# Sources of the cells kept as rows by the first mean pass and loaded by the later ones

## The chip, the cores and the metric

The kernel runs on one core of a Trainium2 chip. The metric is the device time of one execution in microseconds. A core has TensorE (PE in the rows; its weight loads are PEld), VectorE (DVE), ScalarE (ACT), GpSimd (POOL) and the queue engine SyncE (SP), which only issues DMAs here. TensorE's clock has two levels, 1.2 and 2.4 GHz; the granted clock is given as a share of the higher.

## The reference

A graph of 6,250 nodes with 64 features and 206,250 edges sorted by destination goes through four residual blocks, each followed by a layer norm. The first is three mean (SAGE) layers, the second two weighted sums, the third one elementwise sum, the fourth three attention layers. The change touches the three mean layers:

```python
def _sage_conv(x, src, dst, ea, Wl, bl, Wr):
    msg = jax.nn.relu(x[src] + ea)
    s = jax.ops.segment_sum(msg, dst, num_segments=N)
    cnt = jax.ops.segment_sum(jnp.ones((msg.shape[0],), msg.dtype), dst, num_segments=N)
    agg = s / jnp.maximum(cnt, 1.0)[:, None]
    return agg @ Wl + bl + x @ Wr
```

Here ea is edge_attr_16 @ emb_ea, the same in all three layers.

## The kernel before

Nodes are numbered so that source s lies in partition s // 52, column s mod 52 of a table X (later Y) in SBUF. `sage_pass` handles one mean layer. The edges are cut into groups of 896; four groups make a block of destinations. For most edges no row is gathered: the first pass ("sage0", `first_pass` true, 46 blocks) scatters each edge's embedded attributes and its metadata into "bins" in DRAM, one bin for each column of sources, with 112 slots (SL). A *piece* is four such bins (PC = 4) and a block has 13 pieces (NPC = 13). The later passes ("sage1", "sage2", 33 blocks each) read the same bins, and take three further groups a block ("plain" groups) by gathering rows with GpSimd. The first pass has one plain group a block, sums the wide attributes for the third residual block ("aux" events in bodies 2, 4, 6, 9, 11), and does the binning of a block two ahead: binning products in bodies 1, 4, 7, 10 on TensorE, with `pack` on ScalarE, and on VectorE `split` in body 0 and `place` in body 2. It also builds and stores the adjacency that the second residual block uses.

The steps of piece q, body by body of the same loop on every engine (each engine follows its own written order and waits on semaphores):

- ScalarE, `cells_load` (line 1199): the piece's cells (112 slots x 4 bins x 68 words) come from the bins, six pieces ahead (ring RR = 6).
- TensorE, `spread_cells` (line 891): a cell holds the partition of its source, plus 1, as a bf16 number. Four matmuls against the identity put the row of all 448 of them onto all 128 partitions of one of two PSUM banks. In body q the spread of piece q+2 stands in front of everything else.
- VectorE, `near_cells` (line 1034): compares that with the number of the partition and gives the 0/1 matrix `near` (ring R = 3). It stands in body q-1 for piece q, in front of the join.
- TensorE, `fetch` (line 899): four matmuls of `near` and the node table put each cell's source row into PSUM. It waits for near q and for earlier joins (one bank in the first pass, two in the later).
- VectorE, `far_cells` (1038), `join` (1043: fetched rows plus attributes) and, in the first pass, `turned_cells` (1048).
- ScalarE: `rectify` (1204), in the first pass `weigh` (1190, four instructions, needs the join and the turned cells) and `keep` (1210 and its DMA issue 1212) for the adjacency of piece q-2, then the load of the cells of piece q+6.
- TensorE: in the first pass `adjacency` (908) of piece q-2, and `add_cells` (918), which sums the cells of the last pieces. These are gathered in flushes: bodies 0, 3, 7 and 12 of the first pass, 3, 7 and 12 of the later ones.

A plain group (`plain_event`: body 5 in the first pass, 1, 5 and 9 later) adds a product for its attributes (932) and its sums (944) on TensorE, a choice matrix (1062) and a sum (1065) on VectorE in front of that body's join, and a rectifying on ScalarE. SyncE's queue loads sources and attributes.

The first pass's order on ScalarE, in each body:

```python
rectify(qn, s)
if first_pass:
    weigh(qn, k, s)
    if i > 1:
        keep(b, u, it, i - 2)
    elif not (isinstance(b, int) and b == 0):
        keep(*after(b, u, it, -1), NPC + i - 2)
if not (isinstance(b, int) and qn + RR >= pieces):
    cells_load(*spot(b, u, it, i, RR))
```

Of the kernel before, what the change touches and what calls it, by code (L numbers as in the profile page):

```python
# [8 lines left out]
B16 = mybir.dt.bfloat16  # L9
# [5 lines left out]
P = 128  # L15
# [96 lines left out]
def build(nc, A, out):  # L112
    ctx = ExitStack()
    with ctx:
# [12 lines left out]
        adj = dram("adj", (NBK, P, TS * MW))  # L127

# [80 lines left out]
        def lay(region, sizes):  # L209

            at, rings = 0, []
            for n, size in sizes:
# [8 lines left out]
        attr_later = lay(work[:], [(R, PC * SL), (RR, P)])[1]  # L221
# [50 lines left out]
        s_bA = [sem(f"bufA_loaded{i}") for i in range(R)]  # L272
# [9 lines left out]
        s_block = [sem(f"block_loaded{i}") for i in range(2 * NGC)]  # L282
        names = ["bad_counted", "bad_summed", "ids_split", "bins_hot", "bins_counted", "meta_ready", "ranked", "slot_ready", "bin_ea_ready", "pay_ready",
                 "spread", "near_ready", "fetched", "joined", "cells_ready", "far_hot_ready", "weighed", "turned_ready", "adj_ready",
# [462 lines left out]
        def sage_pass(name, table, nodes, B, per, first_pass=False):  # L747
# [5 lines left out]
            ea_banks = [bank[0]]  # L753
# [33 lines left out]
            with nc.Block() as block:  # L787
                @block.sync
                def _(sp):
# [28 lines left out]

                    def body(b, u, it):
                        ahead = after(b, u, it, LEAD)  # L820
                        for i in range(NPC):
                            if first_pass:
# [10 lines left out]
                    if first_pass:  # L833
                        for b in range(LEAD):
                            source_load(b, b)
                            for r in range(GB):
                                bin_load(b, r)
                    for j in range(per):
# [46 lines left out]
                def _(pe):  # L885
                    def spread_cells(qn, b, u, it, i):

                        s, lap = laps(NPC, u, it, i, RR)
                        wait(pe, (s_pays[s], 16 * lap + 16), (q["near_ready"], qn - 1))
# [5 lines left out]
                    def fetch(qn, k, i):  # L895
# [117 lines left out]
                    spread_cells(0, 0, 0, 0, 0)  # L1013
                    spread_cells(1, 0, 0, 0, 1)
# [13 lines left out]
                def _(ve):  # L1028
# [3 lines left out]
                    def near_cells(qn, k):  # L1032
                        wait(ve, (q["spread"], qn + 1), (q["fetched"], qn - R + 1))
                        nc.vector.tensor_scalar(near[k % R], spread[k % 2][:, 0:PC * SL], part1[:], None, ALU.is_equal).then_inc(q["near_ready"].handle, 1)  # L1034
# [97 lines left out]
                    def body(b, u, it):  # L1132
                        ahead = after(b, u, it, LEAD)
                        for i in range(NPC):
# [5 lines left out]
                            if not (isinstance(b, int) and qn == pieces - 1):  # L1140
                                near_cells(qn + 1, k + 1)
# [14 lines left out]
                            if first_pass:  # L1156
                                turned_cells(qn, k, s)

# [5 lines left out]
                    near_cells(0, 0)  # L1164
# [14 lines left out]
                def _(ac):  # L1179
# [33 lines left out]

                    def pack(b, u, r):
# [11 lines left out]
                    def body(b, u, it):  # L1226
# [3 lines left out]
                        for i in range(NPC):  # L1230
# [7 lines left out]
                            if first_pass:  # L1238
# [3 lines left out]
                                elif not (isinstance(b, int) and b == 0):  # L1242
                                    keep(*after(b, u, it, -1), NPC + i - 2)
# [1113 lines left out]
```

## Time and profile before

| | us |
|---|---|
| median of 3 runs | 14045.62 |
| lowest and highest | 14029.52, 14058.77 |
| profiled execution, its own time | 14037.41 |
| span of its profile | 14035.6 |
| mean granted TensorE clock | 0.698 of full |

The page gives busy times over the span and, in 40 slices of 351 us each, busy shares and the granted clock in tenths. Rows of the timeline begin with the start and the duration in us; a bracket at the end says how long the engine was idle before and what released it. Some rows stand for several instructions ("x4"); an f32 matmul counts as two.

### The profile page before, as it was taken

The numbers are of one execution on the slowest core, as the hardware profiler recorded it, in microseconds if no ns is written. First come the engines' busy times: TensorE is split into PE (matmuls) and PEld (weight loads), VectorE is DVE, ScalarE is ACT, GpSimd is POOL, SyncE is SP. The second block draws the span as 40 slices with busy tenths as digits, with TensorE's granted clock in tenths as the row PEclk, the third lists the DMA queues.
The fourth block names the chain that finished last, engine by engine and source line by source line (L and its number), as shares of the span: only waits on it lengthen the run. The fifth ranks groups of instructions, "written<-read, shape, count | busy, mean of one in ns | idle before, by whom it ended". The sixth has DMA issues, their size and how long they took to land. (4 is left out here: it accounts for less than half of the span.)

```text
span 14035.6 us, 291323 instructions
## 1 busy us (share of the span) xinstructions
PE 10475.4 (75%) x76483; PEld 9348.2 (67%) x76484; DVE 8592.3 (61%) x23645; ACT 4454.9 (32%) x9519; POOL 8334.0 (59%) x8516
## 2 busy tenths in 40 slices
PE   5888888888888988788875666666666666666665
PEld 4777777777887878688864555554555554555554
DVE  6666666666656656511136666666666666666666
ACT  2444444441111111100013333333333333333333
POOL 5555555535553645353516777774777774777773
PEclk9988888897988888899975555555555555555555
DMA  4444444432222222376743433332443332443332
GB/s 126 143 140 137 138 143 137 139 112 64 66 64 60 67 63 64 92 256 214 253 137 82 96 94 95 95 94 62 94 95 94 95 94 62 95 95 94 95 94 53
DMA packets 1180716, 1506.22 MB, mean 107 GB/s; under 512 B 379416, under 2 KB 906803, under 8 KB 1179290
## 3 DMA queue, kind: packets, MB, share of 16 engines
q10 hardware_dynamic: 367424, 691.34, 15.4%
q0 software_dynamic: 272384, 301.97, 12.2%
q1 hardware_dynamic: 539610, 498.60, 12.0%
q8 instruction: 448, 7.34, 0.2%
q14 instruction: 850, 6.96, 0.2%
HBM read 1212.18 MB, written 278.84 MB: 106 GB/s over the span
## 5 line engine op out<-in xcount | busy, mean ns | idle before, releaser
L1991 POOL DMA_INDIRECT rows<-gat_table,idx x2457 | 2361.4, 961 | 1309.1 <-issue 747.9
L1991 POOL DMA_INDIRECT Y<-gat_table,idx x2394 | 2305.7, 963 | 729.6 <-issue 729.6
L867 POOL DMA_INDIRECT rows<-node_table,idx x1386 | 1337.9, 965 | 1342.6 <-DVE msg L1065 633.2
L855 POOL DMA_INDIRECT bins<-scratch,slots x1288 | 1336.4, 1038 | 1228.0 <-DVE slots L1115 498.4
L918 PE MATMUL bank<-xT 112*64 112x120 f32 (+1 forms) x11648 | 1575.5, 305 | 0.0
L918 PEld LDWEIGHTS bank<-xT 112*64 112x64 f32 (+1 forms) x11648 | 1513.0, 164 | 17.3
L1204 ACT ACTIVATE xT<-xT 112x256 f32<-112x256 f32 x1456 | 604.2, 415 | 2892.8 <-DVE xT L1043 2526.8
L2005 PE MATMUL scores<-ident,rep 128*128 128x128 f32 x2436 | 600.9, 424 | 1123.1 <-ACT rep L2096 826.8
L2005 PE MATMUL scores<-ident,scratch 128*128 128x128 f32 x2415 | 595.8, 424 | 1075.3 <-ACT scratch L2096 863.0
L2050 PE MATMUL bank<-sel,msg 128*72 128x32 f32 x9702 | 1308.7, 309 | 0.0
L2005 PEld LDWEIGHTS scores<-ident,rep 128*128 128x128 f32 x2436 | 471.6, 222 | 1169.5 <-issue 1169.5
L2050 PEld LDWEIGHTS bank<-sel,msg 128*72 128x72 f32 x9702 | 1215.8, 237 | 44.4
L2005 PEld LDWEIGHTS scores<-ident,scratch 128*128 128x128 f32 x2415 | 467.6, 222 | 1121.5 <-issue 1121.5
L2152 DVE CUSTOM_DVE_ANT_0 work<-scores,work 128x896 f32<-128x896 f32 x1041 | 1108.0, 1089 | 104.5 <-PE scores L2005 23.0
L1043 DVE TENSOR_TENSOR xT<-scores,xT 112x256 f32<-112x256 f32 x1028 | 434.9, 423 | 1081.7 <-PE scores L899 1053.2
L1327 POOL DMA_INDIRECT rows<-node_table,idx x658 | 623.1, 947 | 769.0 <-DMA idx<-in_src 280.9
L1038 DVE TENSOR_TENSOR xT<-counts,xT 112x480 f32<-112x480 f32 x1456 | 949.3, 652 | 203.7 <-PE bank L918 168.4
L1034 DVE TENSOR_SCALAR work<-scores,part 128x448 f32<-128x448 f32 x1456 | 987.9, 678 | 34.3 <-PE scores L891 34.3
L908 PE MATMUL bank<-xT,work 112*128 112x120 f32 x4784 | 791.0, 317 | 212.0 <-ACT work L1210 178.3
L908 PEld LDWEIGHTS bank<-xT,work 112*128 112x128 f32 x4784 | 702.3, 223 | 350.3 <-issue 343.9
L899 PE MATMUL scores<-X,work 128*112 128x64 f32 x4784 | 654.0, 286 | 255.1 <-issue 250.0
L891 PE MATMUL scores<-ident,xT 112*128 112x112 bf16 x5824 | 556.6, 221 | 301.7 <-DVE work L1034 182.5
(249 smaller groups left out, 21439.8 us busy)
## 6 DMA issues: line engine op xcount, KB each, us to landing
work<-in_dst_rows SPq DMA_DIRECT2D x693, 448.0 KB
xT<-bins ACTq DMA_DIRECT2D x1456, 119.0 KB
adj<-work ACTq DMA_DIRECT2D x598, 240.0 KB
work<-adj ACTq DMA_DIRECT2D x184, 780.0 KB, 4.4
xT<-adj ACTq DMA_DIRECT2D x184, 780.0 KB
bins<-zeros ACTq DMA_DIRECT2D x46, 1547.0 KB, 8.2
work<-in_attr SPq DMA_DIRECT2D x231, 224.0 KB
work<-in_dst_rows SPq DMA_DIRECT2D x693, 64.0 KB
```

The source lines that it names most:

```text
L855: nc.gpsimd.indirect_dma_start(bins, bass.IndirectOffsetOnAxis(slots[u % 2][:, r * G + j:r * G + j + 1], 0), binf[r][:, j, :], None).then_ ...
L867: nc.gpsimd.indirect_dma_start(rows[s][:, k, 0:D], None, table, bass.IndirectOffsetOnAxis(idx[s][:, k:k + 1], 0)).then_inc(s_rows[s].handl ...
L899: last = nc.tensor.matmul(joint[k % JR][0:SL, c * D:(c + 1) * D], near[k % R][:, c * SL:(c + 1) * SL], nodes[:, i * PC + c, :], start=True ...
L908: last = nc.tensor.matmul(adj_sum[:, c * MW:(c + 1) * MW], turned[k % R][0:SL, c * P:(c + 1) * P], far_hot[k % RR][0:SL, c * MW:(c + 1) * ...
L918: last = nc.tensor.matmul(sums[u % SR][0:width, 0:MW], cellf[k % RR][0:SL, c, 0:width], far_hot[k % RR][0:SL, c * MW:(c + 1) * MW], start= ...
L1034: nc.vector.tensor_scalar(near[k % R], spread[k % 2][:, 0:PC * SL], part1[:], None, ALU.is_equal).then_inc(q["near_ready"].handle, 1)
L1038: nc.vector.tensor_tensor(far_hot[s][0:SL, :].rearrange("p (c m) -> p c m", m=MW), bc(counts[0:SL, 1:MW + 1], [SL, PC, MW], 1), bc(payf[s] ...
L1327: nc.gpsimd.indirect_dma_start(rows[s][:, k, 0:D], None, table, bass.IndirectOffsetOnAxis(idx[s][:, k:k + 1], 0)).then_inc(s_rows[s].handl ...
L1991: nc.gpsimd.indirect_dma_start(rows[s][:, j, :], None, gat_table, bass.IndirectOffsetOnAxis(idx[s % RR][:, j:j + 1], 0)).then_inc(s_rows[s ...
L2005: last = nc.tensor.transpose(score_banks[s % 2][:, j * P:(j + 1) * P], reps[s % 2][:, j, :], ident[:])
L2050: last = nc.tensor.matmul(wide[s % 2][0:ROW, 0:WIN], msg[s % R][:, j, :], sel[s % R][:, j, :], start=j == 0, stop=j == G - 1)
L2152: nc.vector.tensor_tensor_reduce(out=fars[s % 2][k], in0=score_banks[s % 2][:, 0:GE], in1=fars[s % 2][k], scale=1.0, scalar=-3.0e38, op0=A ...
```

## The change

The first pass copies, for each piece, partition 0 of the spread bank as bf16 to SBUF on ScalarE (`keep_row`) and stores that row (448 numbers of two bytes, 896 bytes) to a new DRAM tensor `sources`. The bank may be spread over only when its row is copied: `spread_cells` waits for `row_out_ready` too. The copy for piece q+1 stands in ScalarE's body q behind `keep` and in front of the cells' load.

The later passes have no `spread_cells`. SyncE's queue loads the stored row onto all 128 partitions (`row_load`, ring of six, issued when near q-6 is done), and `near_cells` reads it from SBUF. It now stands behind the join of body q, for piece q+2. The freed PSUM bank becomes a second bank for the plain groups' attribute products. The rest is bookkeeping of semaphores.

```diff
+        sources = dram("sources", (NBK, TS * SL // 2))
...
+        kept_row = [work[0:1, (3 * R - 1) * GE + i * PC * SL // 2:(3 * R - 1) * GE + (i + 1) * PC * SL // 2] for i in range(R)]
+        attr_later, row = lay(work[:], [(R, PC * SL), (RR, P), (RR, PC * SL // 2)])[1:]
...
-            ea_banks = [bank[0]]
+            ea_banks = [bank[0]] if first_pass else [bank[0], bank[1]]
...
+                    def row_load(b, u, it, i):
+                        qn = NPC * b + i
+                        s, lap = laps(NPC, u, it, i, RR)
+                        wait(sp, (q["near_ready"], qn - RR + 1))
+                        sp.dma_start(row[s], sources[ds(b, 1), i * PC * SL // 2:(i + 1) * PC * SL // 2].broadcast_to([P, PC * SL // 2])
+                                     ).then_inc(s_row[s].handle, 16)
...
                         for i in range(NPC):
+                            if not first_pass and not (isinstance(b, int) and NPC * b + i + RR >= pieces):
+                                row_load(*spot(b, u, it, i, RR))
...
-                        wait(pe, (s_pays[s], 16 * lap + 16), (q["near_ready"], qn - 1))
+                        wait(pe, (s_pays[s], 16 * lap + 16), (q["near_ready"], qn - 1), (q["row_out_ready"], qn - 1))
...
-                            if not (isinstance(b, int) and qn + 2 >= pieces):
+                            if first_pass and not (isinstance(b, int) and qn + 2 >= pieces):
                                 spread_cells(qn + 2, *spot(b, u, it, i, 2))
-                            fetch(qn, k, i)
+                            fetch(qn, b, u, it, i)
...
-                        wait(ve, (q["spread"], qn + 1), (q["fetched"], qn - R + 1))
-                        nc.vector.tensor_scalar(near[k % R], spread[k % 2][:, 0:PC * SL], part1[:], None, ALU.is_equal).then_inc(q["near_ready"].handle, 1)
+                        wait(ve, (q["spread"], qn + 1) if first_pass else (s_row[s], 16 * lap + 16), (q["fetched"], qn - R + 1))
+                        found = spread[k % 2][:, 0:PC * SL] if first_pass else row[s].bitcast(B16)
+                        nc.vector.tensor_scalar(near[k % R], found, part1[:], None, ALU.is_equal).then_inc(q["near_ready"].handle, 1)
...
                             far_cells(qn, s, lap)
-                            if not (isinstance(b, int) and qn == pieces - 1):
-                                near_cells(qn + 1, k + 1)
+                            if first_pass and not (isinstance(b, int) and qn == pieces - 1):
+                                near_cells(qn + 1, *spot(b, u, it, i, 1))
...
                             join(qn, k, s)
                             if first_pass:
                                 turned_cells(qn, k, s)
+                            elif not (isinstance(b, int) and qn + 2 >= pieces):
+                                near_cells(qn + 2, *spot(b, u, it, i, 2))
...
+                    def keep_row(b, u, it, i):
+                        qn, k = NPC * b + i, NPC * u + i
+                        s, lap = laps(NPC, u, it, i, R)
+                        wait(ac, (q["near_ready"], qn + 1), (s_row_kept[s], 16 * lap))
+                        nc.scalar.activation(kept_row[s].bitcast(B16), spread[k % 2][0:1, 0:PC * SL], ACT.Copy).then_inc(q["row_out_ready"].handle, 1)
+                        wait(ac, (q["row_out_ready"], qn + 1))
+                        ac.dma_start(sources[ds(b, 1), i * PC * SL // 2:(i + 1) * PC * SL // 2], kept_row[s]).then_inc(s_row_kept[s].handle, 16)
...
                                     keep(*after(b, u, it, -1), NPC + i - 2)
+                                if not (isinstance(b, int) and qn == pieces - 1):
+                                    keep_row(*spot(b, u, it, i, 1))
                             if not (isinstance(b, int) and qn + RR >= pieces):
                                 cells_load(*spot(b, u, it, i, RR))
```

## Rows read from the trace of the kernel before

**Rows 1.** The page: busy times over the span; granted TensorE clock by slice.

```profile
PE 10475.4 (75%) x76483; PEld 9348.2 (67%) x76484; DVE 8592.3 (61%) x23645; ACT 4454.9 (32%) x9519; POOL 8334.0 (59%) x8516
...
PEclk9988888897988888899975555555555555555555
```

**Rows 2.** Line 1034 in each mean pass: min/median/max ns, first and last start.

```profile
L1034 DVE TENSOR_SCALAR work<-scores,part x598: 670/679/684, 123.4 to 3095.0; 128x448 f32<-128x448 f32 x200
...
L1034 DVE TENSOR_SCALAR work<-scores,part x429: 670/679/683, 3221.1 to 4493.2; 128x448 f32<-128x448 f32 x143
...
L1034 DVE TENSOR_SCALAR work<-scores,part x429: 668/679/685, 4539.3 to 5834.6; 128x448 f32<-128x448 f32 x143
```

**Rows 3.** Timeline of TensorE in a block of the first pass: start, duration.

```profile
1513.67 1.71 PE L899 MATMUL scores<-X,work 128*112 128x64 f32 x8
1515.32 1.70 PE L977 MATMUL bank<-scratch,work 128*64 128x32 f32 x14
1516.95 2.06 PE L908 MATMUL bank<-xT,work 112*128 112x120 f32 x8
1518.81 0.58 PE L891 MATMUL scores<-ident,xT 112*128 112x112 bf16 x4
1519.18 1.71 PE L899 MATMUL scores<-X,work 128*112 128x64 f32 x8
1521.13 2.03 PE L908 MATMUL bank<-xT,work 112*128 112x120 f32 x8 [0.24 <-ACT work L1210]
...
1526.84 0.96 PE L899 MATMUL scores<-X,work 128*112 128x64 f32 x8
```

**Rows 4.** Timeline of VectorE in that block: joins of bodies 0, 2, 3, 4, 12, 0.

```profile
1507.86 0.42 DVE L1043 TENSOR_TENSOR xT<-scores,xT 112x256 f32<-112x256 f32 x1 [0.26 <-DVE Y L1108]
...
1518.00 0.42 DVE L1043 TENSOR_TENSOR xT<-scores,xT 112x256 f32<-112x256 f32 x1 [0.17 <-DVE maxrank L1117]
...
1521.07 0.42 DVE L1043 TENSOR_TENSOR xT<-scores,xT 112x256 f32<-112x256 f32 x1 [0.37 <-PE scores L899]
...
1527.98 0.42 DVE L1043 TENSOR_TENSOR xT<-scores,xT 112x256 f32<-112x256 f32 x1 [4.72 <-PE scores L899]
...
1559.84 0.43 DVE L1043 TENSOR_TENSOR xT<-scores,xT 112x256 f32<-112x256 f32 x1 [3.29 <-PE scores L899]
...
1573.89 0.42 DVE L1043 TENSOR_TENSOR xT<-scores,xT 112x256 f32<-112x256 f32 x1 [0.26 <-DVE Y L1108]
```

**Rows 5.** Timeline of ScalarE in body 2 of that block.

```profile
1519.15 1.28 ACT L1190 ACTIVATE work<-work,xT 112x128 f32<-112x128 f32 x4 [0.18 <-DVE work L1048]
1520.33 0.55 ACT L1210 ACTIVATE work<-bank 128x480 f32<-128x480 f32 x1
1521.12 0.37 ACTq L1212 DMA_DIRECT2D adj<-work  x1
1521.73 0.33 ACTq L1199 DMA_DIRECT2D xT<-bins  x1
```

**Rows 6.** Windows of that block: length, busy PE, PEld, DVE, ACT, POOL, clock, DMA, GB/s.

```profile
1516.00:1520.00 4.00, 4.00 (x27) 3.89 (x26) 3.79 (x7) 1.27 (x4) 1.28 (x1) 0.50 0.54 160
...
1552.00:1556.00 4.00, 2.94 (x35) 2.79 (x35) 3.02 (x7) 2.58 (x8) 1.39 (x1) 1.00 0.35 108
1556.00:1560.00 4.00, 3.93 (x21) 3.72 (x22) 0.68 (x3) 2.04 (x6) 2.87 (x3) 0.52 0.63 192
```

**Rows 7.** Timeline of TensorE in a block of the second mean pass.

```profile
4200.80 0.37 PE L891 MATMUL scores<-ident,xT 112*128 112x112 bf16 x4
...
4206.93 0.36 PE L891 MATMUL scores<-ident,xT 112*128 112x112 bf16 x4 [1.14 <-DVE work L1034]
...
4208.01 5.16 PE L918 MATMUL bank<-xT 112*64 112x120 f32 x32
```

**Rows 8.** Timeline of VectorE in the same stretch.

```profile
4205.20 0.42 DVE L1043 TENSOR_TENSOR xT<-scores,xT 112x256 f32<-112x256 f32 x1
...
4206.11 0.68 DVE L1034 TENSOR_SCALAR work<-scores,part 128x448 f32<-128x448 f32 x1
```

More of the change, by code:

```diff
@@ L271, in build @@
         s_idx = [sem(f"idx_loaded{i}") for i in range(RR)]
-        s_bA = [sem(f"bufA_loaded{i}") for i in range(R)]
+        s_bA = [sem(f"bufA_loaded_or_row_kept{i}") for i in range(R)]
+        s_row_kept = s_bA
         s_rows = [sem(f"rows_loaded{i}") for i in range(GR)]
@@ L281, in build @@
         s_kept = [sem(f"adjacency_kept{i}") for i in range(R)]
-        s_block = [sem(f"block_loaded{i}") for i in range(2 * NGC)]
+        s_block = [sem(f"stored_piece_loaded{i}") for i in range(2 * NGC)]
+        s_row = s_block[0:RR]
         names = ["bad_counted", "bad_summed", "ids_split", "bins_hot", "bins_counted", "meta_ready", "ranked", "slot_ready", "bin_ea_ready", "pay_ready",
-                 "spread", "near_ready", "fetched", "joined", "cells_ready", "far_hot_ready", "weighed", "turned_ready", "adj_ready",
+                 "spread", "row_out_ready", "near_ready", "fetched", "joined", "cells_ready", "far_hot_ready", "weighed", "turned_ready", "adj_ready",
                  "adj_out_ready", "cells_summed", "accumulated", "auxsel_ready",
@@ L837, in _ @@
                                 bin_load(b, r)
+                    else:
+                        for i in range(RR):
+                            row_load(0, 0, 0, i)
                     for j in range(per):
@@ L893, in spread_cells, with fetch @@
                         last.then_inc(q["spread"].handle, 1)
-                    def fetch(qn, k, i):
+                    def fetch(qn, b, u, it, i):
+                        k = NPC * u + i
                         wait(pe, (q["near_ready"], qn + 1), (q["joined"], qn - JR + 1))
@@ L1012, in _ @@
                                 bin_event(b, b, r)
-                    spread_cells(0, 0, 0, 0, 0)
-                    spread_cells(1, 0, 0, 0, 1)
+                        spread_cells(0, 0, 0, 0, 0)
+                        spread_cells(1, 0, 0, 0, 1)
                     over_blocks(body, B)(pe.Fori)
@@ L1163, in _ @@
                             place(b, b)
-                    near_cells(0, 0)
+                    near_cells(0, 0, 0, 0, 0)
+                    if not first_pass:
+                        near_cells(1, 0, 0, 0, 1)
                     over_blocks(body, B)(ve.Fori)
@@ L1254, in _ @@
                         cells_load(0, 0, 0, i)
+                    if first_pass:
+                        keep_row(0, 0, 0, 0)
                     over_blocks(body, B)(ac.Fori)
@@ L1264, in _ @@
                             ac.wait_ge(s_kept[i].handle, s_kept[i].at(16 * slot_total(i, R, pieces)))
+                            ac.wait_ge(s_row_kept[i].handle, s_row_kept[i].at(16 * slot_total(i, R, pieces)))
             for s in range(RR):
@@ L1269, in sage_pass @@
                 s_pays[s].done(16 * slot_total(s, RR, pieces))
+                if not first_pass:
+                    s_row[s].done(16 * slot_total(s, RR, pieces))
             for s in range(AR):
                 s_attr[s].done(16 * slot_total(s, AR, n1))
-            for x in ["spread", "near_ready", "fetched", "joined", "cells_ready", "far_hot_ready", "cells_summed"]:
+            for x in (["spread", "row_out_ready"] if first_pass else []) + ["near_ready", "fetched", "joined", "cells_ready", "far_hot_ready", "cells_summed"]:
                 q[x].done(pieces)
@@ L1279, in sage_pass @@
                     s_kept[s].done(16 * slot_total(s, R, pieces))
+                    s_row_kept[s].done(16 * slot_total(s, R, pieces))
                 s_ve.done((6 + 3 + 3) * B)
```

5 lines of the change are left out of this document (3 added, 2 removed).

## The prediction

> **What bounds the kernel now.** I read the page first [rows 1]: TensorE is busy for 75% of the span, and its granted clock is near full in the first 18 slices, which hold the three mean passes, and at half in the attention passes behind them, which the change leaves alone. Then I dated the passes by the instruction that finds the near cells, line 1034 [rows 2]: 598 pieces from 123 to 3095 us in the first pass, 429 from 3221 to 4493 in the second, 429 from 4539 to 5835 in the third. That is 64.6 us for each of the 46 blocks of the first pass and 38.5 and 39.2 us for each of the 33 blocks of the others. The rest of the forecast is about what a block costs.
>
> Next I laid one block of the first pass beside its engines. The joins (line 1043, VectorE) are the mark to count by, one for each piece: 1507.86 is body 0 and 1573.89 is body 0 of the next block, 66.0 us [rows 4]. No engine bounds it throughout. From body 12 to body 0 (1559.84 to 1573.89, 14.05 us [rows 4]) VectorE is at the split; in the bodies that flush, TensorE is at its sums (to body 4's fetch, 1519.18 to 1526.84 [rows 3]); in the others the four engines hand a piece on in about 3 us. What makes 3 us possible is that the engines work on different pieces: TensorE spreads piece q+2 and fetches q while ScalarE is still weighing q-1.
>
> In a later block TensorE has nearly all the time, but with a wait: it spreads piece 7 at 4206.93 only when near (line 1034) has let it, after 1.14 us idle [rows 7].
>
> **The change in the first pass.** Every piece gets a copy of one row to SBUF on ScalarE and one more DMA issue. That ScalarE has room (32% of the span busy [rows 1]) is not the question; the new wait is. TensorE may spread piece q+2 only when ScalarE has copied piece q's row (two spread banks), and it does so ahead of fetch q. ScalarE copies row q at the end of its body q-1: behind the rectify, the weighing and the keeping of that body, all of which hang on join q-1, which hangs on fetch q-1. So fetch q now waits for a chain that begins with fetch q-1, and the pieces no longer overlap. The loop, from join to join:
> - join to weigh start, 1518.00 to 1519.15: 1.15 [rows 4, 5]
> - weigh to keep, 1519.15 to 1520.33: 1.18 [rows 5]
> - keep to its DMA issue, to 1521.12: 0.79 [rows 5]
> - from there to the next slot, where now the cells' load is issued (1521.73) and where the row's copy will stand: 0.61 [rows 5]
> - the copy, 448 elements a partition out of PSUM: the nearest row is the keep's 480, 0.55; the one partition saves nothing that I count [rows 5]
> - to TensorE's next start: keep's end (1520.33 + 0.55) to the adjacency at 1521.13, 0.25 [rows 3, 5]
>
> Sum 4.53 us from a join to the next spread. Then spread to fetch, 0.37 at half clock (1518.81 to 1519.18 [rows 3]), 0.2 at full; fetch to join 1.89 at half (1519.18 to 1521.07) and 1.14 at full (1526.84 to 1527.98) [rows 3, 4]. Join to join is 5.87 us at full clock and 6.79 us at half, where it was about 3. The copy's own DMA issue and the cells' load behind it take some 1.4 us more (0.79 and 0.61 again) and end before the next rectify can start, so they cost nothing; if the chain were shorter than 4 us they would.
>
> A block has 13 such gaps. The one from body 12 to body 0 stays 14.05: the split needs only the spread of piece 1 and the first sums of the flush, and both come as before.
> - All at full clock: 12 x 5.87 + 14.05 = 84.5, and an estimated 2.5 for the placing and the plain group, which hold VectorE longer than a loop: 87 us.
> - All at half: 12 x 6.79 + 14.05 = 95.5. In seven bodies an aux or binning product lies between fetch and adjacency: fetch 1513.67, aux 1515.32, adjacency 1516.95 for 2.06 [rows 3], so keep can begin 3.28 + 2.06 + 0.25 = 5.6 us behind the fetch, not 1.89 + 2.33 = 4.22: 7 x 1.4 = 9.6. The flushes of bodies 3 and 7 hold TensorE beyond the loop (1519.18 to a spread at 1526.84 - 0.2, 7.46 us against 1.89 + 4.53 = 6.4 [rows 3]), about 1 and 3 us, less 1.8 as the clock is up behind them; the plain group 2. Together 109 us.
>
> Which clock? From 1516 to 1520 TensorE was busy all 4 us and still had 0.50; between 1552 and 1556 it was busy 2.94 of 4 and the next stretch has 0.52 [rows 6]. In the new loop a body outside the flushes gives TensorE half of 0.37 + 1.65 + 2.06, with an aux product half of 1.63 more [rows 3]: 2.0 to 2.9 us of work at full clock in 5.9, a smaller share than in the stretch ahead of that fall. I take half clock for about four gaps in five, the flushes lifting it for a body or so: 109 - 0.2 x 22 = 104 to 105, say 104. Less 66.0 is 38 us a block, and x 46 that is **+1750 us**. Bounds: +21 a block at full clock (+970); +50 (+2300) if the falls also reach what I leave unchanged.
>
> The clock is also where a rule of the skill gives another sum. The Trainium skill, TensorE: Matmul & The Clock Gate, section "HAM oscillation", lays a lost clock at gaps of idleness longer than one that it names, and the gaps of this loop would stay just under it; by it the block would be the 87 us one. This trace doesn't bear it out where the clock falls behind a stretch that was three quarters busy, so it stays a rival.
>
> The 598 stores are one row of 896 bytes each, and their slot is waited for only three pieces later, some 18 us; nothing.
>
> **The change in the later passes.** Each piece loses its four spreading matmuls and gains a load on SP's queue, asked for six pieces ahead (over 15 us), so I take it as hidden; the group loads behind it on that queue now go out about one block ahead rather than as soon as their slot is free, and a block is 35 us: hidden too. If the load came late, near would wait for DMA, and I have no row for its landing; by the bound of the cells' load, which has as many bytes and is six ahead too, nothing shows. Near goes behind the join and two pieces ahead. VectorE has the same instructions; near's source is now SBUF, priced as before.
>
> One group of four bodies now takes from 4200.80 to 4208.01, 7.21 us [rows 7]. Without spreads TensorE's work up to fetch 6 is over 0.6 us sooner. The last fetch then waits for near 7: the join of 5 at 4205.20 [rows 8] comes 0.4 sooner (two spreads), near starts 0.34 behind it, as far did, instead of 0.91 (4206.11 [rows 8]), and takes 0.68; the old wait ran 0.82 from near's start (4206.11 to 4206.93 [rows 7, 8]) and a spread of 0.2. So flush starts at 7.21 - 0.4 - 0.57 - 0.2 = 6.04. That is 1.17 less a group, 3.5 a block, and x 66 blocks **-230 us**. Bounds: 0, if the clock takes it back; -420, if all 13 spreads and the waits of 1.14 go (6.4 x 66).
>
> **Sum.** +1750 - 230 = +1520. On the profiled execution (span 14035.6, its time 14037.4) that is 15,560; the median of the runs shown is 8 us above it, which is nothing here. **15,560 us.**
>
> **The rivals.**
> - *The loop at full clock*, or at a good part of it: +970 - 230, from about 14,750 up to 15,300. For it: flushes lift the clock quickly. Against: [rows 6]. 27%.
> - *The copy is absorbed* (the other side): ScalarE is idle for about half of those stretches [rows 6], and if the row's copy came in that idle time without TensorE waiting for it, the first pass would stay and 230 us be won: 13,800. It would decide so wherever the wait on the copy is met before the join of the same body. Against: the copy's place in ScalarE's order, behind rectify and keep. 7%.
> - *Worse than the half-clock loop*: the block nearer 116, or nothing won later on: above 16,050. 6%.
> - *No effect*, by the two halves cancelling: they differ by seven times. 1%.
> - *My forecast*, loop mostly at half clock: 15,300 to 16,050. 59%.
>
> **How the numbers follow.** The range 14,750 to 16,050 holds the forecast's own and the full-clock rival's cases, about 85 in 100; what is left out is the other side and the worst case. 0.2% (28 us) is about what a measurement of this kernel can tell from no change. Slower by more than that 0.92, within it 0.01, faster 0.07.
>
> **What would show it.** Right: joins of the first pass 6 to 8 us apart outside the split; TensorE's spread (line 891's successor) idle in front, released by ScalarE's new copy, some 2 to 3 us each in 598; the first pass ending near 4840 us; clock there down from 8 or 9 tenths to 6 or 7; later blocks near 35.5 us with no 1.14 us waits. Wrong: a spread that waits for nothing; a first pass that ends where it did; later passes that wait for the row's DMA. What would make the sum wrong with the mechanism right is the clock, by up to 700 us.

## Result, and the profile after

Before 14,047.67 us (14,029.52 to 14,058.77, 4 runs), after 15,402.83 us (15,399.27 to 15,407.38, 4 runs): 1.0966 times before, 95% interval 1.0947 to 1.0985, or 1355 us slower. The forecast was 15,560.

The page after, first the busy times, then the granted clock by slice, as [rows 1]:

```profile
PE 11014.5 (72%) x73051; PEld 9786.3 (64%) x73052; DVE 8385.4 (54%) x23645; ACT 4820.0 (31%) x10117; POOL 8307.6 (54%) x8516
...
PEclk7666666666666998998999655555555555555555
```

TensorE has 3,432 matmuls fewer and is busy for 539 us longer: its work was done at a lower clock. The 12 slices at 6 tenths lie in the first pass. Line 1055 (near cells, line 1034 before) in the three passes, to set against [rows 2]; min/median/max ns, first and last start:

```profile
L1055 DVE TENSOR_SCALAR work<-scores,part x598: 669/676/684, 123.2 to 4856.0; 128x448 f32<-128x448 f32 x200
...
L1055 DVE TENSOR_SCALAR work<-work,part x429: 435/444/552, 4988.5 to 6072.1; 128x448 f32<-128x448 bf16 x143
...
L1055 DVE TENSOR_SCALAR work<-work,part x429: 436/444/642, 6117.1 to 7194.2; 128x448 f32<-128x448 bf16 x143
```

From first to last near cells the passes take 4732.8, 1083.6 and 1077.1 us, against 2971.6, 1272.1 and 1295.3. That is +1761 in the first pass and -188.5 and -218.2 in the later ones, in sum +1354 of the 1362 us between the two profiled spans: almost the whole difference lies here.

How the +1761 of the first pass splits for TensorE is in its windows, with the second pass below. First the kernel before, then after; columns are length, busy us (instructions) of PE, PEld, DVE, ACT, POOL, granted clock, DMA share, GB/s:

```profile
123.00:3095.00 2972.00, 2491.22 (x20990) 2286.74 (x20988) 2025.19 (x3777) 1351.65 (x3969) 1675.53 (x1586) 0.87 0.47 139
3221.00:4493.00 1272.00, 1142.40 (x10087) 1033.50 (x10087) 778.32 (x1611) 234.66 (x526) 670.98 (x693) 0.88 0.28 65
```

```profile
123.00:4856.00 4733.00, 3328.44 (x20985) 3017.78 (x20984) 2031.39 (x3777) 1714.51 (x4565) 1574.73 (x1586) 0.64 0.28 87
4988.00:6072.00 1084.00, 1001.92 (x8376) 894.20 (x8377) 671.67 (x1610) 234.52 (x525) 705.17 (x693) 0.91 0.54 122
```

The same 21,000 matmuls of the first pass are busy for 3328 us instead of 2491 (+837: the clock went from 0.87 to 0.64), and TensorE is idle for 1405 us instead of 481 (+924: the wait).

The loop itself, from one join to the next (after, the timeline of all engines; start and duration in us, in brackets the idle time before):

```profile
1935.57 0.42 DVE L1064 TENSOR_TENSOR xT<-scores,xT 112x256 f32<-112x256 f32 x1 [4.37 <-PE scores L917]
...
1936.73 1.28 ACT L1215 ACTIVATE work<-work,xT 112x128 f32<-112x128 f32 x4 [0.18 <-DVE work L1069]
...
1936.96 2.06 PE L926 MATMUL bank<-xT,work 112*128 112x120 f32 x8
...
1939.17 0.57 ACT L1235 ACTIVATE work<-bank 128x480 f32<-128x480 f32 x1 [1.17 <-PE bank L926]
1939.98 0.36 ACTq L1237 DMA_DIRECT2D adj<-work  x1
1940.62 0.53 ACT L1243 ACTIVATE work<-scores 1x448 bf16<-1x448 f32 x1 [0.87 <-ACT work L1235]
...
1941.25 0.53 PE L907 MATMUL scores<-ident,xT 112*128 112x112 bf16 x4 [2.23 <-issue]
...
1941.57 1.71 PE L917 MATMUL scores<-X,work 128*112 128x64 f32 x8
...
1943.46 0.42 DVE L1064 TENSOR_TENSOR xT<-scores,xT 112x256 f32<-112x256 f32 x1 [5.48 <-PE scores L917]
```

Join to weigh 1.16, weigh to keep 2.44 (1.17 of it a wait for the adjacency product), keep to its DMA issue 0.81, to the copy 0.64, copy to spread 0.63, spread to fetch 0.32, fetch to join 1.89: 7.89 us, each step in the place that the prediction gave it (6.79, and 1.4 more where an aux or binning product lies between, as here). The gap before this one, from a join at 1929.02, has no wait for the adjacency and is 6.55.

### The profile page after: what moved, and what is told of

It reads as the page before. It is cut to its first block and busy times, and to the rows that moved or that the text cites. A ratio compares the mean times of both kernels' runs of the same rounds, so it can differ in the third digit from the quotient of the medians.

```text
span 15397.5 us, 290993 instructions
## 1 busy us (share of the span) xinstructions
PE 11014.5 (72%) x73051; PEld 9786.3 (64%) x73052; DVE 8385.4 (54%) x23645; ACT 4820.0 (31%) x10117; POOL 8307.6 (54%) x8516
## 5 line engine op out<-in xcount | busy, mean ns | idle before, releaser
L871 POOL DMA_INDIRECT bins<-scratch,slots x1288 | 1282.4, 996 | 3000.3 <-ACT scratch L1251 1575.2
L883 POOL DMA_INDIRECT rows<-node_table,idx x1386 | 1410.3, 1018 | 933.8 <-DMA idx<-in_src 508.3
L936 PE MATMUL bank<-xT 112*64 112x120 f32 (+1 forms) x11648 | 1540.3, 300 | 0.0
L907 PE MATMUL scores<-ident,xT 112*128 112x112 bf16 x2392 | 280.9, 260 | 1413.3 <-issue 1112.5
L907 PEld LDWEIGHTS scores<-ident,xT 112*128 112x128 bf16 x2392 | 180.0, 116 | 1519.6 <-issue 1518.4
L926 PEld LDWEIGHTS bank<-xT,work 112*128 112x128 f32 x4784 | 975.9, 296 | 156.8 <-issue 143.1
L926 PE MATMUL bank<-xT,work 112*128 112x120 f32 x4784 | 1054.3, 392 | 1.0 <-ACT work L1235 1.0
L1368 POOL DMA_INDIRECT rows<-node_table,idx x658 | 624.2, 949 | 723.8 <-DVE msg L1417 247.8
L917 PE MATMUL scores<-X,work 128*112 128x64 f32 x4784 | 890.3, 356 | 0.0
```

Of the source, the lines that this page charges most:

```text
L871: nc.gpsimd.indirect_dma_start(bins, bass.IndirectOffsetOnAxis(slots[u % 2][:, r * G + j:r * G + j + 1], 0), binf[r][:, j, :], None).then_ ...
L883: nc.gpsimd.indirect_dma_start(rows[s][:, k, 0:D], None, table, bass.IndirectOffsetOnAxis(idx[s][:, k:k + 1], 0)).then_inc(s_rows[s].handl ...
L917: last = nc.tensor.matmul(joint[k % JR][0:SL, c * D:(c + 1) * D], near[k % R][:, c * SL:(c + 1) * SL], nodes[:, i * PC + c, :], start=True ...
L926: last = nc.tensor.matmul(adj_sum[:, c * MW:(c + 1) * MW], turned[k % R][0:SL, c * P:(c + 1) * P], far_hot[k % RR][0:SL, c * MW:(c + 1) * ...
L936: last = nc.tensor.matmul(sums[u % SR][0:width, 0:MW], cellf[k % RR][0:SL, c, 0:width], far_hot[k % RR][0:SL, c * MW:(c + 1) * MW], start= ...
L1368: nc.gpsimd.indirect_dma_start(rows[s][:, k, 0:D], None, table, bass.IndirectOffsetOnAxis(idx[s][:, k:k + 1], 0)).then_inc(s_rows[s].handl ...
```

## Experiments

**One copy, three places in ScalarE's order.** The first run moves the copy, with its store, to the head of ScalarE's body, ahead of pack, rectify and weigh; all else of the change stays.

```diff
                             s, lap = laps(NPC, u, it, i, RR)
+                            if first_pass and not (isinstance(b, int) and qn == pieces - 1):
+                                keep_row(*spot(b, u, it, i, 1))
                             if first_pass and i in at_bin and binned_ahead(b):
...
-                                if not (isinstance(b, int) and qn == pieces - 1):
-                                    keep_row(*spot(b, u, it, i, 1))
```

> The changed kernel with one thing moved: ScalarE copies and stores the row of piece q+1 first in its body q, ahead of packing, rectifying and weighing; the same work, off the chain that begins with the join. If the loop through the copy is the cost (first pass 123 to 4856 us in the changed kernel, 102.9 us a block), the loop is gone and only some 1.3 us more of ScalarE's work in each body is left, which shows in the dense bodies: about 72 us a block, first pass ending near 3450 us, total 13,900 to 14,050. If ScalarE's added work itself, or the store, is the cost, nothing moves: 15,400.

Measured 14,066.81 us, 1.0006 times before (0.9997 to 1.0016): no difference from before, 8.7% less than the change as made, and 17 us above the range expected. The first pass takes 3392 us instead of 4733, the later passes 1084.0 and 1083.2, as after. The 1341 us hang on one place in an order. The second run puts the same two lines between weigh and keep.

```diff
                                 weigh(qn, k, s)
+                                if not (isinstance(b, int) and qn == pieces - 1):
+                                    keep_row(*spot(b, u, it, i, 1))
...
                                     keep(*after(b, u, it, -1), NPC + i - 2)
-                                if not (isinstance(b, int) and qn == pieces - 1):
-                                    keep_row(*spot(b, u, it, i, 1))
```

> The copy of the row between weighing and keeping: still behind the join, but the chain is shorter by keep, its DMA issue and the way to the copy, 0.79 + 0.58 = 1.37 us a body, and by the wait of keep for the adjacency where there is one. If the loop is the cost: 12 bodies x 46 blocks x 1.37 = 760 us less, up to 1200 with those waits, a little less where a flush holds TensorE: 14,300 to 14,800. If the work is the cost, or if only being ahead of the join helps: 15,400.

Measured 14,532.14 us, 1.0341 times (1.0312 to 1.0370); first pass 3847 us, clock 0.70. The nearer the copy stands to the head of the body, the shorter the pass: 4733, 3847, 3392.

**More work, no more waiting.** If the price were ScalarE's own time, more of it would cost more. This run has ScalarE copy 448 zeros on one partition twice more in each body of the first mean pass, behind the cells' load, where nothing on TensorE waits for it; nobody reads the result.

```diff
+                    ac_spare = work[0:1, 3 * R * GE - PC * SL // 2:3 * R * GE].bitcast(B16)
...
                                 cells_load(*spot(b, u, it, i, RR))
+                            if first_pass:
+                                for n in range(2):
+                                    wait(ac, (s_ac, 2 * qn + n))
+                                    nc.scalar.activation(ac_spare, zeros[0:1, 0:PC * SL], ACT.Copy).then_inc(s_ac.handle, 1)
```

> The changed kernel with two further one-partition copies of 448 numbers on ScalarE behind the cells' load of every body of the first pass (about 1.2 us, more than the row's copy with its issue adds); nobody waits for them. If the wait and not the work is the cost, they fall into ScalarE's idle 1.5 to 2 us ahead of the next rectify: 15,400, within 0.4%. If ScalarE's work is the cost: 598 x 1.2 = +700, 16,100.

Measured 15,414.5 us, 1.0974 times (1.0946 to 1.1002), as after. Its windows of the first pass:

```profile
124.00:4855.00 4731.00, 3330.65 (x20983) 3021.90 (x20983) 2031.18 (x3776) 2391.43 (x5757) 1570.41 (x1585) 0.64 0.29 87
```

ScalarE is busy for 677 us more (2391 against 1715) and the pass is no longer: ScalarE's throughput is not what costs.

**How much is the clock.** TensorE gets 24 small matmuls (bf16, 64 columns, into a bank nobody reads) ahead of its wait for the copy, in 11 of 13 bodies: the wait stays, but TensorE is busy in part of it.

```diff
+FILL = 24
...
+                        if (i + NPC - 2) % NPC not in (9, 10) and not (isinstance(qn, int) and qn < 13):
+                            for _ in range(FILL):
+                                nc.tensor.matmul(bank[6][:, 448:512], ident16[:], ident16[:, 0:64], start=True, stop=True)
                         wait(pe, (s_pays[s], 16 * lap + 16), (q["near_ready"], qn - 1), (q["row_out_ready"], qn - 1))
```

> The changed kernel with 24 small bf16 matmuls (64 columns) into unused columns of the plain groups' bank ahead of the wait of each spread in the first pass, in 11 of 13 bodies; their result is read by nobody. It asks how much of the 102.9 us a block is TensorE's lower clock (0.63 of full in a block of the changed kernel). If the fillers hold the clock up, a block falls towards the 87 us of the full-clock sum, less what they cost where nothing is waited for: 92 to 98 us, total 14,900 to 15,200. If the clock stays at half whatever is done, they add their own time in the flushing bodies: 15,450 to 15,700.

Measured 15,199.22 us, 1.0816 times (1.0786 to 1.0846), at the upper end of what was expected.

```profile
124.00:4650.00 4526.00, 3476.03 (x32861) 3214.99 (x32861) 2033.90 (x3777) 1714.22 (x4565) 1606.88 (x1585) 0.73 0.30 91
```

With 11,900 matmuls more the pass is 206 us shorter, at a clock of 0.73 instead of 0.64. So the clock is a price of its own beside the wait. By the prediction's blocks of 87 and 109 us full against half clock would be 1012 us over 46 blocks. The clock rose by 0.09 of the 0.50 that lie between the two levels, which would be 182 us, estimated, and 206 were found, the filler's own time included. A clock near full was not reached, so the whole share of the clock stays an estimate.

**The later passes: order or spreads.** They gained 407 us where 230 were forecast. The first run puts near cells back in front of the join, one piece ahead, as before the change; row loads stay, spreads stay away.

```diff
-                            if first_pass and not (isinstance(b, int) and qn == pieces - 1):
+                            if not (isinstance(b, int) and qn == pieces - 1):
                                 near_cells(qn + 1, *spot(b, u, it, i, 1))
...
-                            elif not (isinstance(b, int) and qn + 2 >= pieces):
-                                near_cells(qn + 2, *spot(b, u, it, i, 2))
...
-                    if not first_pass:
-                        near_cells(1, 0, 0, 0, 1)
```

> The changed kernel with near of the later passes back where it was, one piece ahead and in front of the join; the row still comes from SBUF and there are no spreads. It asks what the order is worth of the 406 us that the two later passes fell (1272 to 1084 and 1295 to 1077 us from first to last near). The prediction's account gives the order 0.57 us a group of bodies, 198 groups: +110 us, 15,510. If the order is worth nothing (TensorE bound): 15,400.

Measured 15,611.19 us, 1.1102 times (1.1085 to 1.1119). The later passes are 1173.5 and 1180.2 us, 193 more than after: the order is worth 193, not the 110 expected. How much the passes as changed vary by themselves, six profiles show: in the change and in the five runs that leave these passes alone and in which the kernel before took its 14,050 us, their sum lies between 2160.7 and 2178.5 us. The 193 are against the lowest of them. The second run has TensorE make the spreads in the later passes as before, with no wait on near or copy; nobody reads them.

```diff
-            ea_banks = [bank[0]] if first_pass else [bank[0], bank[1]]
+            ea_banks = [bank[0]]
...
-                        wait(pe, (s_pays[s], 16 * lap + 16), (q["near_ready"], qn - 1), (q["row_out_ready"], qn - 1))
+                        wait(pe, (s_pays[s], 16 * lap + 16), *([(q["near_ready"], qn - 1), (q["row_out_ready"], qn - 1)] if first_pass else []))
...
-                            if first_pass and not (isinstance(b, int) and qn + 2 >= pieces):
+                            if not (isinstance(b, int) and qn + 2 >= pieces):
                                 spread_cells(qn + 2, *spot(b, u, it, i, 2))
```

> The changed kernel with the four spreading matmuls a piece still made in the later passes and read by nobody (and one bank for the plain groups' attributes, as before the change); near reads the row from SBUF, in its new place. If TensorE's time is most of the gain: 858 x 0.2 = +170 us, up to +240 with the half clock in part of it: 15,570 to 15,640. If the gain is all in VectorE's shorter near and the order: within 40 us of 15,400.

Measured 15,392.19 us, 1.0943 times (1.0927 to 1.0960): the first case, with TensorE's time as most of the gain, is a miss; the time measured is that of the second. The later passes take 1077.9 and 1064.2, in sum 2142, 19 us less than the lowest of the six without the spreads. Why, the groups of TensorE in the second pass show; first before, then after, then this run (matmuls, busy us, mean ns, idle before them):

```profile
L918 PE MATMUL bank<-xT 112*64 112x120 f32 x3384 | 480.3, 315 | 0.0
...
L891 PE MATMUL scores<-ident,xT 112*128 112x112 bf16 x1712 | 160.0, 217 | 128.6 <-DVE work L1034 90.5 <-issue 37.7 <-DMA xT<-bins 0.3
```

```profile
L936 PE MATMUL bank<-xT 112*64 112x120 f32 x3384 | 425.2, 292 | 0.0
L917 PE MATMUL scores<-Y,work 128*112 128x64 f32 x1712 | 219.8, 274 | 47.6 <-DVE work L1055 39.6 <-issue 8.0
L917 PE MATMUL bank<-Y,work 128*112 128x64 f32 x1710 | 218.8, 273 | 39.1 <-DVE work L1055 39.1
```

```profile
L936 PE MATMUL bank<-xT 112*64 112x120 f32 x3384 | 374.4, 270 | 0.0
L917 PE MATMUL scores<-Y,work 128*112 128x64 f32 x1719 | 212.6, 268 | 14.0 <-DVE work L1055 11.3 <-issue 0.2
L917 PE MATMUL bank<-Y,work 128*112 128x64 f32 x1712 | 211.4, 268 | 19.0 <-DVE work L1055 17.1
L907 PE MATMUL scores<-ident,xT 112*128 112x112 bf16 x1712 | 160.2, 216 | 17.5 <-issue 16.5 <-DMA xT<-bins 1.0
```

The spreads fill stretches in which TensorE else waits for near (idle before the fetches 87 us after, 33 here), and the same 3384 products of the sums take 270 ns instead of 292: the clock is 0.97 in these passes, 0.91 and 0.92 after. In the second pass TensorE is busy for 76 us more outside the sums, 51 less in them, and idle for 31 less. In this order a spread costs nothing.

**A version faster than before?** The next three runs start from the copy at the head. The first has SyncE issue the row's store, one piece ahead, behind the attribute loads of its body.

```diff
+                    def row_store(b, u, it, i):
...
+                        wait(sp, (q["row_out_ready"], qn + 1))
+                        sp.dma_start(sources[ds(b, 1), i * PC * SL // 2:(i + 1) * PC * SL // 2], kept_row[s]).then_inc(s_row_kept[s].handle, 16)
...
+                            if first_pass and not (isinstance(b, int) and NPC * b + i == pieces - 1):
+                                row_store(*spot(b, u, it, i, 1))
...
-                        wait(ac, (q["row_out_ready"], qn + 1))
-                        ac.dma_start(sources[ds(b, 1), i * PC * SL // 2:(i + 1) * PC * SL // 2], kept_row[s]).then_inc(s_row_kept[s].handle, 16)
```

> The copy first in the body, as in the experiment that only moves it, and the store's DMA issued by SyncE's queue and not by ScalarE's, which saves ScalarE about 0.5 us a body. If ScalarE's work shows in dense bodies once the loop is gone: 80 to 200 us below that experiment, 13,750 to 13,900. If ScalarE is not the bound there: no difference.

Measured 14,075.53 us, 1.0012 times (1.0003 to 1.0021): no difference from the copy at the head, whose first pass took 3392 us and this one's 3396. But two waits for late attributes, which that run does not have, appear in its list of waits between 500 and 3000 us (total, times, longest):

```profile
PE bank L1005 <- DMA work<-in_attr: 176.2, 98, 2.6
...
PE scores L996 <- DMA work<-in_attr: 51.0, 37, 2.0
```

SyncE, it seems, now stands at the store's wait, and the attribute loads behind it go out late. The next run issues each store five bodies later, when its copy is long done:

```diff
+                            if first_pass and not (isinstance(b, int) and NPC * b + i < 4):
+                                row_store(*spot(b, u, it, i, -4))
...
+                    if first_pass:
+                        for i in range(NPC - 4, NPC):
+                            row_store(B - 1, (B - 1) % UB, (B - 1) // UB, i)
```

> The copy first in ScalarE's body and the store on SyncE's queue, but five pieces further back in that queue's order, so that the attribute loads behind it go out early again (with the store one piece ahead TensorE waited 1.5 to 2.3 us at 1567.55, 1588.07, 1592.71 and 1619.86 for DMA of the attributes). If those waits ate what ScalarE's shorter body saved: first pass about 3150 to 3280 us instead of 3396, total 13,800 to 13,950, faster than the kernel before. If ScalarE's 0.5 us a body is worth nothing: as before the move, 14,060.

It ran, with two of those below, on chip 13, on which the kernel before itself took 18,076 us instead of 14,050, so these are compared only with each other and with that. It took 18,287.22 us, 1.0124 times (1.0101 to 1.0148). The same kernel once more, on chip 6:

> The kernel with the copy first and the store five pieces back on SyncE's queue, once more, since in its first call the kernel before itself took 18,076 us and not 14,047. As expected then: first pass about 3150 to 3280 us, total 13,800 to 13,950, if the late attribute loads ate what ScalarE's shorter body saved; 14,060 if that half microsecond is worth nothing.

There before took 18,368 us and it took 18,550.16, 1.0101 times (1.0078 to 1.0125). The waits for the attributes are gone from the list of waits of the same stretch, as the reading of SyncE's queue wants it, but others, which the trace puts down to no instruction of the core, stand on VectorE (up to 16.4 us) and ScalarE (up to 14.5), with the other engines behind them:

```profile
DVE xT L1075 <- remote: 838.0, 86, 16.4
```

On both of these chips it is 1% slower than the kernel before; what it takes on one without such waits stays open. No version here was shown to beat the kernel before.

**What is left of the later passes.** Near reads bf16 from SBUF now and takes 0.444 us instead of 0.678. This run cuts it in two halves of 0.331 each in the later passes, together about the old duration; all else is as in the change.

```diff
+                            half_row = PC * SL // 2
+                            nc.vector.tensor_scalar(near[k % R][:, 0:half_row], found[:, 0:half_row], part1[:], None, ALU.is_equal)
+                            nc.vector.tensor_scalar(near[k % R][:, half_row:], found[:, half_row:], part1[:], None, ALU.is_equal).then_inc(q["near_ready"].handle, 1)
```

> The changed kernel with near of the later passes in two instructions of 224 columns, which brings its time on VectorE from 0.44 back to about the 0.68 us that it took from PSUM; place and order as changed. If near's price is on the path (TensorE waits 79 us a pass for it in the changed kernel, 130 times): two nears a group, 198 groups, 0.2 us each: +40 to +80 us, 15,440 to 15,490. If it is hidden: 15,400.

Measured 19,675.74 us, 1.0874 times (1.0841 to 1.0908). It ran on chip 13. Here and in the next two runs the passes are dated from first to last join. Its later passes take 3168.7 us; those of the store-behind run on the same chip, which are the change's own, 3142.7: +26 for the old duration, less than the 40 to 80 expected. The same passes took 3219.4 on chip 6, and the six runs of the store-behind kernel on chip 13 lie up to 155 us apart, so 26 from one profile each can't be told from nothing. The last two are one kernel, run on chip 13 and on chip 6, with the two edits shown above, near back in its old place and the spreads made:

> Both at once: spreads of the later passes still made, and near back in its old place; what is left of the change there is near's source (SBUF, 0.44 instead of 0.68 us, and no wait on a spread). The later passes took 2567 us before, 2354 with near in the old place and no spreads, 2142 with near in the new place and spreads made, 2161 as changed. If the spreads cost nothing in either order, the later passes take about 2350 and the total is 15,600; if they cost TensorE's 0.2 us a piece when it waits for near more often: 2350 + 170, total 15,780.

> Near in its old place and the spreads still made, once more for the same reason. If the spreads cost nothing in either order, the later passes take about 2350 us and the total is 15,600, and what is left of the gain, some 210 us, belongs to near's source (0.44 instead of 0.68 us, and no wait on a spread); if they cost TensorE's 0.2 us a piece: 2350 + 170, total 15,780.

Measured 19,825.67 us, 1.0965 times (1.0940 to 1.0991), and 20,088.61, 1.0935 times (1.0910 to 1.0961). Against the store-behind kernel on the same chip the later passes take +220 and +173 us, where the old place alone cost 193: with near in its old place too the spreads cost about nothing. What they do cost is within the 25 or so by which these two miss 193 on either side, and that is no more than the noise here.

## Why the prediction was right, and where its sizes were off

**The loop: right, and shown.** Moving the copy with its store, and nothing else, gives back 1341 of the 1761 us; more work on ScalarE costs nothing. In the block read above joins lie 6.5 to 9.1 us apart outside the split: the ten gaps from 1905.24 to 1981.88 average 7.66 us, and the gap at the split is 13.80 against 14.05. A block takes 102.9 in the mean against 104 forecast, and the pass ends at 4856 against 4840. TensorE's wait in front of the spread is there, but the trace names "issue" for most of it. The groups of the first pass after, TensorE's spread and ScalarE's copy:

```profile
L907 PE MATMUL scores<-ident,xT 112*128 112x112 bf16 x2389 | 280.6, 260 | 1404.6 <-issue 1112.5 <-ACT work L1243 292.0
```

```profile
L1243 ACT ACTIVATE work<-scores 1x448 bf16<-1x448 f32 x596 | 317.7, 533 | 480.0 <-ACT work L1235 462.9 <-issue 13.8 <-DVE work L1055 3.3
```

All 1405 us of TensorE's idle time stand before the spread. Forecast were 2 to 3 us at each of the 598; 465 spreads waited, 3.0 us each in the mean, and the others found TensorE at work, so it is 2.3 us a piece over all. Only 292 are put down to the copy. The timeline settles it: 457 of the 465 start within 0.3 us behind a copy's end, most of them 0.1 (1941.15 and 1941.25 above), and the runs that move the copy move the idle time. The copy's price, too, was right: one partition of 448 elements takes 0.53 us, as 480 on 128 partitions take 0.56.

**The clock: right.** Windows of the same block after, and the row of TensorE that the fall belongs to:

```profile
1920.00:1922.00 2.00, 2.00 (x21) 1.47 (x20) 2.00 (x4) 1.30 (x5) 0.00 (x0) 1.00 0.01 1
1922.00:1924.00 2.00, 0.57 (x6) 0.39 (x4) 1.00 (x4) 1.30 (x4) 1.45 (x2) 1.00 0.52 132
1924.00:1926.00 2.00, 1.25 (x10) 1.28 (x10) 0.00 (x0) 0.53 (x1) 1.52 (x2) 0.71 0.41 149
1926.00:1928.00 2.00, 2.00 (x6) 1.32 (x6) 0.00 (x0) 0.00 (x0) 1.57 (x2) 0.50 0.61 136
```

```profile
1924.75 0.48 PE L907 MATMUL scores<-ident,xT 112*128 112x112 bf16 x4 [2.18 <-issue]
```

TensorE is at 2.4 GHz until it has waited 2.18 us for the copy, and at 1.2 GHz from then on, through the bodies up to the next flush. A mean of 0.64 is full speed for 28% of the time; the forecast had half clock in four gaps of five, with flushes above it. The rival by the Trainium skill (TensorE: Matmul & The Clock Gate, "HAM oscillation"), a clock kept up because each gap of the loop is shorter than the one it names, put the block at 87 us. The trace disagrees: a gap of 2.18 us came ahead of the fall here, and the measured block is 102.9. The kernel before shows it with a gap half as long, ahead of the fall in [rows 6]:

```profile
1555.95 1.83 PE L908 MATMUL bank<-xT,work 112*128 112x120 f32 x8 [1.06 <-DVE xT L1038]
```

**The absorbed copy: wrong for the change, right as a mechanism.** Met before the join of the same body, the wait nearly vanishes, as that rival said. But the pass stays 421 us longer than before, not equal. The same matmuls are busy for 2798 us there instead of 2491 (clock 0.79), and TensorE is idle for 594 instead of 481: 307 of the 421 go with the clock and 114 with waits. The windows of the pass, and TensorE's spread in it, to set against the same line before the change:

```profile
124.00:3516.00 3392.00, 2797.72 (x20973) 2545.23 (x20974) 2030.40 (x3776) 1657.68 (x4562) 1638.36 (x1585) 0.79 0.41 121
```

```profile
L907 PE MATMUL scores<-ident,xT 112*128 112x112 bf16 x2384 | 246.7, 235 | 126.0 <-issue 107.5 <-ACT work L1243 15.1 <-DVE work L1055 0.5
```

```profile
L891 PE MATMUL scores<-ident,xT 112*128 112x112 bf16 x2391 | 233.6, 225 | 15.6 <-issue 15.3 <-DVE work L1034 0.4
```

TensorE's idle time ahead of the spread is 126 us, against 16 before and 1405 in the change: these 110 are nearly all of the 114. That they start the falls of the clock is argued, not shown: no run took the copy out of the way altogether, and other short waits of this pass (249 us ahead of the adjacency product, 210 before the change) may do it too.

**The later passes: right in sign and in the group of four, mis-sized in the sum.** The group of [rows 7] after, the two fetches around the wait, and two sums:

```profile
5518.54 1.00 PE L917 MATMUL scores<-Y,work 128*112 128x64 f32 x8
...
5523.57 0.97 PE L917 MATMUL bank<-Y,work 128*112 128x64 f32 x8 [0.58 <-DVE work L1055]
5524.47 3.50 PE L936 MATMUL bank<-xT 112*64 112x120 f32 x32
5527.89 1.00 PE L917 MATMUL scores<-Y,work 128*112 128x64 f32 x8
```

Group start to flush is 5.93 us, 6.04 forecast, 7.21 before; the last fetch waits for near, as forecast, 0.58 us where the forecast's terms come to about 0.8. With near in its old place it is 6.50, so the order's 0.57 was exact in this group (in the sums, too, that run is slower: 303 ns instead of 292 in the second pass):

```profile
5514.98 1.00 PE L917 MATMUL scores<-Y,work 128*112 128x64 f32 x8
...
5520.58 0.97 PE L917 MATMUL bank<-Y,work 128*112 128x64 f32 x8 [1.14 <-DVE work L1055]
5521.48 3.50 PE L936 MATMUL bank<-xT 112*64 112x120 f32 x32
```

A block takes 32.8 and 32.6 us in the two passes, not the 35.5 forecast. The term that was mis-sized is "1.17 less a group, 3.5 a block, and x 66 blocks": it takes the flush as unchanged. The flush of 32 products took 5.16 us at 4208.01 and takes 3.50 here, but the next flush of the same block before, at 4220.32, took 3.49 already, so that pair shows more than the mean; over a pass the same 3384 took 480 us and take 425 (315 and 292 ns), which is 55 of the second pass's 188.5. The other 133 are 85 of busy time outside the sums and 48 of idle time, from the windows of that pass: busy 1142.4 and 1002.0, idle 129.6 and 81.6. The 85 are what 428 spreads of 0.2 us come to. Yet the price of the spreads failed as well: the 0.4 us of TensorE's time that the prediction gave them in each group (79 us in 198 groups) came back as nothing when they were put in again, since the sums and the waits shrank by as much. Near's source, priced as before, was 0.23 us cheaper; what that is worth was not told from nothing (26 us). And the bound of -420 is mis-added: 13 spreads of 0.2 and three waits of 1.14 are 6.0 us a block, not 6.4, which gives -400; the -407 lie beyond it.

So of 407 us, 193 go with the order and none with the spreads' time alone, nor with the second bank for the attributes, which the run with the spreads gave up too. What is left, 214, falls to near's shorter duration and to the coupling that went with the spreads (near waiting for a spread in TensorE's order, and that spread for an earlier near), with the clock that it cost. That is found by subtraction only, and across chips: no run brings back the coupling alone, so its cause stays open. The row loads were hidden, as said: DMA share went from 0.28 to 0.54, and the four waits for them come to 13 us in both passes.

**The sum.** First pass +1761 against +1750, later passes -407 against -230: the 157 us between forecast and result are the later passes' almost alone (177 more won there than forecast, 11 more lost in the first pass).

## What to carry to other kernels

A short instruction on an engine with room can cost several times its own duration if another engine's in-order queue waits for it: ask behind what it stands, and whether that hangs on what the waiter did just before. Here 0.53 us at the end of a body cost 2.9 us a piece, and at its head 0.7. And before taking small work from TensorE, see what it fills: if the engine only waits in that time, nothing may be won; here the clock was 0.97 with the spreads and 0.91 without.

## What the runs showed of the hardware

- Matmuls that nobody needs, put where TensorE would be idle, made passes shorter twice: clock 0.64 to 0.73 and 206 us less with a filler, 0.91 to 0.97 and 19 us less with unread spreads. (The last is one profile against six that lie 18 us apart among themselves, and too little for the total time to tell.)
- The compare of 128 x 448 took VectorE 0.444 us from bf16 in SBUF and 0.678 from f32 in PSUM, both to f32; cut in halves, 2 x 0.331.
- The kernel before took about 14,050 us in three measurements, on chips 0 and 8 among others, and 18,076 and 18,368 us on chips 13 and 6, where the version with the store behind shows waits of up to 16 us that no instruction of the core ends; why is open. The copy's place still cost there (on chip 13, from first to last join, first passes of 5531 and 5522 us with it at the end of the body, 4152 with it at the head).
- TensorE's clock fell to 1.2 GHz behind a wait of 2.18 us that followed busy stretches at full clock, and in the kernel before behind one of 1.06 us.
